# Chunk 0's phase A in two passes, and every second FFN weight cast on VectorE

## The reference

```python
# 1: mamba (inner width 2048)
xc, z = split(x @ W_in)                      # W_in 1024 x 4096
u  = silu(causal_conv4(xc))                  # per channel, 4 taps
dt_raw, B_raw = split(u @ W_x)               # 16 + 16 columns
dt = clip(softplus(dt_raw @ W_dt + b_dt), 1e-4, 1.0)
h_t = h_{t-1} * (1 - dt_t) + u_t * (B_raw @ W_Bp)_t
out = ((h + D_param * u) * silu(z)) @ W_out
# 2 and 4: ffn; the weights are int32 in -127..127, times 1/127, hidden width 3072
out = (silu(x @ wg.T) * (x @ wu.T)) @ wd.T
# 3: causal attention with K, V = split(x @ W.T), q = x, and its own residual
out = x + softmax(x @ K.T + mask) @ V
```

## Time and profile before

| | us |
|---|---|
| runs of the kernel | 3325.86, 3313.39; median 3319.63 |
| the profiled execution | 3315.65 |
| its span, first to last instruction, slowest core (core 1) | 3314.1 |
| spans of the 8 cores | 3288.6 to 3314.1 |
| busy: PE 1987.4, PE weight load 969.5, VectorE 954.4, ScalarE 776.3, GpSimd 323.3 | |

### The profile page before, as it was taken

One profiled execution on the slowest core, in us unless ns is written; L12 is line 12 of the kernel. 1 busy time (PEld: TensorE's weight loads), 2 busy tenths in 40 slices (PEclk: granted clock), 3 DMA queues, 4 the chain that ended last, 5 costly groups with the idle time before them and its releaser, 6 DMA issues.

```text
span 3314.1 us, 30059 instructions; the slowest of 8 cores (3288.6 to 3314.1 us)
## 1 busy us (share of the span) xinstructions
PE 1987.4 (60%) x9432; PEld 969.5 (29%) x9432; DVE 954.4 (29%) x1617; ACT 776.3 (23%) x1196; POOL 323.3 (10%) x404
## 2 busy tenths in 40 slices
PE   0355555555555531385776759514988486859587
PEld 0233333333333310131332324211434232324232
DVE  3244444444444440020211211053443121211121
ACT  0244545445454423300110101010011200101010
POOL 0222222122222210013000000000000000000000
PEclk9777666776767755697788989856999698989889
DMA  7200000000000018615112030344041512030303
GB/s 236 89 13 26 1 26 1 26 26 1 26 1 26 22 37 257 202 62 183 29 51 76 25 103 4 121 152 133 1 134 58 187 39 89 16 111 0 118 10 99
DMA packets 69851, 233.31 MB, mean 70 GB/s; under 512 B 8450, under 2 KB 8578, under 8 KB 67652
## 3 DMA queue, kind: packets, MB, share of 16 engines
q10 hardware_dynamic: 35712, 112.21, 10.2%
q1 hardware_dynamic: 27460, 91.92, 9.1%
q0 software_dynamic: 6528, 27.27, 2.0%
HBM read 170.55 MB, written 60.82 MB: 70 GB/s over the span
## 4 chain that ended last, share of the span: by engine, by line
PE 38%; DMA 22%; DVE 12%; ACT 9%; issue 8%; DVEq 4%; POOLq 3%; POOL 2%; ACTq 2%; SPq 0%
PE ps_s L974 15%; DMA arena<-wd_c 7%; PE ps_s L940 5%; DVEq L143 4%; DMA arena<-xs 4%; PE ps_s L1044 3%; PE ps L1044 3%; POOLq L143 2%; ACT L679 2%; POOL arena L560 2%; PE ps_s L1296 2%; DVE arena L516 2%; PE ps L759 2%; PE ps_s L1222 2%; DMA arena<-wu_t 2%
## 5 line engine op out<-in xcount | busy, mean ns | idle before, releaser
L974 PE MATMUL ps_s<-arena 128*128 128x512 bf16 x2304 | 511.7, 386 | 6.3 <-DVE arena L328 6.3
L584 PE MATMUL ps_s<-arena 128*128 128x256 bf16 x1024 | 214.1, 397 | 388.6 <-ACT arena L508 388.6
L318 PE MATMUL ps<-arena 128*128 128x128 bf16 x512 | 63.5, 307 | 488.7 <-DVE arena L307 488.7
L974 PEld LDWEIGHTS ps_s<-arena 128*128 128x128 bf16 x2304 | 228.1, 99 | 288.6 <-issue 25.8
L1044 PE MATMUL ps_s<-arena 128*128 128x512 bf16 x768 | 213.3, 401 | 135.9 <-DMA arena<-wd_c 89.4
L266 ACT ACTIVATE arena<-arena 128x1024 bf16<-128x1024 f32 x64 | 67.6, 1057 | 913.7 <-DMA arena<-xs 823.6
L584 PEld LDWEIGHTS ps_s<-arena 128*128 128x128 bf16 x1024 | 136.8, 138 | 458.0 <-issue 406.0
L940 PE MATMUL ps_s<-arena 128*128 128x512 bf16 x768 | 171.6, 387 | 122.2 <-ACT arena L950 63.5
L989 DVE TENSOR_TENSOR arena<-arena,ps_s 128x512 bf16<-128x512 f32 x144 | 99.0, 687 | 423.2 <-ACT arena L983 423.2
L1044 PE MATMUL ps<-arena 128*128 128x512 bf16 x768 | 212.5, 400 | 0.0
L499 PE MATMUL ps_s<-arena 128*128 128x256 bf16 x1024 | 163.2, 328 | 65.2 <-DVE arena L447 64.6
(11 more groups left out here) (93 smaller groups left out, 2347.7 us busy)
## 6 DMA issues: line engine op xcount, KB each, us to landing
xs<-arena ACTq DMA_DIRECT2D x48, 512.0 KB, 2.9
arena<-xs ACTq DMA_DIRECT2D x48, 512.0 KB, 4.3
arena<-wd_c SPq DMA_DIRECT2D x84, 256.0 KB, 2.6
arena<-wd_c ACTq DMA_DIRECT2D x84, 256.0 KB, 2.6
arena<-wg_t SPq DMA_DIRECT2D x16, 768.0 KB, 6.6
arena<-wu_t SPq DMA_DIRECT2D x16, 768.0 KB, 6.7
arena<-x ACTq DMA_DIRECT2D x16, 512.0 KB, 4.7
arena<-w_in ACTq DMA_DIRECT2D x8, 1024.0 KB, 10.6
```

What stands on the lines that cost most here:

```text
L318: lambda e, s=xn_bf_tile, dj=dj, pbf=pbf: e.transpose(pbf[:, dj * P:(dj + 1) * P], s[:, dj * P:(dj + 1) * P], g_ident),
L584: lambda e, dj=dj, ci=ci, bkx=bkx, half=half, par=par: e.matmul(psb[bkx][:, half * TCM:(half + 1) * TCM], win_bf[:, dj * 4096 + ci * P: dj ...
L974: lambda e, hi=hi, dj=dj, bk=bk, par=par, wsrc=wsrc: e.matmul(psb[bk], wsrc[:, dj * H + hi * P: dj * H + (hi + 1) * P], fxnt[par][:, dj * ...
```

## The change

Two edits. First, in chunk 0 all eight xc pairs of phase A are emitted, and then all eight z pairs. Second, while the gate and up weights are staged, the pieces of slot 1 are cast by VectorE (`tensor_copy`) and those of slot 0 by ScalarE as before. VectorE's cast waits for its load and for the ScalarE cast of slot 0 that goes with it, and SP's loads and GpSimd's stores then wait for VectorE's mark where they waited for ScalarE's.

```diff
         for p in range(8):
             phaseA_xc_pair(0, p)
-            phaseA_z_pair(0, p)
+        for zp in range(8):
+            phaseA_z_pair(0, zp)
         mk_xz_last = s_pe.mark()
         xp_sec(0)
         mamba_load_ln(1)
...
-                            em.op("scalar",
-                                  lambda e, dj=dj, hh=hh, dstw=dstw, slot=slot: e.copy(
-                                      dstw[:, dj * H + hh * 1536: dj * H + (hh + 1) * 1536],
-                                      stg[slot][:]),
-                                  wait=[mkd], inc=[(s_se, 1)], drain=False)
-                            prev2[slot] = mkk[dj] = s_se.mark()
+                            if slot == 0:
+                                em.op("scalar",
+                                      lambda e, dj=dj, hh=hh, dstw=dstw, slot=slot: e.copy(
+                                          dstw[:, dj * H + hh * 1536: dj * H + (hh + 1) * 1536],
+                                          stg[slot][:]),
+                                      wait=[mkd], inc=[(s_se, 1)], drain=False)
+                                prev2[slot] = s_se.mark()
+                            else:
+                                em.op("vector",
+                                      lambda e, dj=dj, hh=hh, dstw=dstw, slot=slot: e.tensor_copy(
+                                          dstw[:, dj * H + hh * 1536: dj * H + (hh + 1) * 1536],
+                                          stg[slot][:]),
+                                      wait=[mkd, prev2[0]], inc=[(s_ve, 1)],
+                                      drain=False)
+                                prev2[slot] = s_ve.mark()
+                            mkk[dj] = prev2[slot]
                             prev_cast[0] = mkk[dj]
```

## The result

| | before | changed |
|---|---|---|
| median of all runs | 3313.65 us (42 runs) | 3322.97 us (43 runs) |
| ratio | | 1.0027, 95% interval 1.0017 to 1.0038 |
| profiled execution, slowest core's span | 3314.1 us | 3315.3 us (core 4) |

The change makes the kernel slower by 0.27%, 8.9 us of 3313.65, with an interval from 5.6 to 12.6 us. The forecast was 6.1 us more, 0.18%. By the 2% bound it is no change.

A forecast was written before the change was run, and what follows sets the result against it. No single limit: a serial chain bounds phase A of chunk 0, transfers the weight stage. +9.6 us (first edit) and -3.5 (second) make +6.1, on the median of two runs, 3319.63, giving 3325.7 us; range 3311 to 3340.

The forecast's parts named there:

- The xc part: Phase A, chunk 0: an xc pair costs 5.95 us, 0.47 less than before; 3.7 us gained by the eighth SiLU.
- The z part without cover: Phase A, chunk 0: six z pairs left with nothing beside them; 11.4 us lost at full clock.
- clock term: Phase A, chunk 0: the z part begins at 1.2 GHz and loses 1.9 us, about half of such a stretch.
- No slack behind it: After phase A of chunk 0: chunk 1's loads, LayerNorm, transposes and first phase B matmul follow, so nothing absorbs the delay.
- (c): Rival: the first edit costs nothing, chunk 1's loads or the chunk behind having slack; -3.5 us in all; 5%.
- The cast on VectorE: Weight staging: a VectorE cast takes 0.96 us, 0.51 less than ScalarE's; 2 us counted of 7.7.
- 2 won and 2 lost: Weight staging: 2 us gained by the faster cast (0 to 7.7), 2 lost by slot 1's late first cast (0 to 4.7).
- The end of the stage: Weight staging: gate-phase SiLUs wait only for ScalarE's last cast, now slot 0's, so PE starts 3.45 us earlier.
- (a): Rival: weight staging is paced by latency, the shorter cast pays in full, -9.1 us there, +0.5 in all; 15%.
- (b): Rival: chunk 0's whole z part runs at 1.2 GHz, +17.7 us there, +14.2 in all; 12%.
- (d): Rival: both staging slots fall into step and the DMA engines idle during cast pairs; up to 55 us; 4%.
- (e): Rival: VectorE's casts wait and end no earlier than ScalarE's; +9.6 us stays, second edit near 0; 10%.

The follow-up runs named there:

- e2: The kernel before with only the second edit, slot 1's casts on VectorE, first run; ratio 0.9961 (0.9931 to 0.9990).
- e12: The kernel before with only the second edit, slot 1's casts on VectorE, run again; ratio 0.9986 (0.9966 to 1.0005).
- e5: The kernel before with all 16 casts of w_up on VectorE and all 16 of w_gate on ScalarE; ratio 0.9873 (0.9857 to 0.9888).
- e3: Second edit alone, but the first two casts both stay on ScalarE; edit against e2; ratio 0.9965 (0.9930 to 1.0001).
- e8_z_first_all: The kernel before with, in all 8 chunks, the z pair emitted ahead of its xc pair's last SiLU; ratio 0.9736 (0.9722 to 0.9749).

## Why the prediction was right

**The xc part: right.** 5.95 us a pair was predicted, 5.92 to 5.93 measured. The saving of one z SiLU per pair is real: the eighth L570 came 41.5 us after the first, 45.4 before, 3.9 us gained where 3.7 was forecast.

**The z part without cover: right, with luck in its clock term.** From the eighth L570 to the loads of x it takes 15.3 us on the core shown (162.98 to 178.32) where it took 1.2. As the mean of the cores it is 14.5 us, 13.3 more than before, and that is the 11.4 + 1.9 of the sum. The 1.9 was half of one row's low stretch. In the 32 blocks of the four kernels with edit 1 the low stretch lasts 2.9 to 6.1 us (matmuls start 0.21 us apart in it, 0.11 behind it) and costs 1.4 to 2.9 us. The reason that was given for it is off: the forecast took PE in the xc part for as thinly used as in the stretch from 1180, 1.91 of 5.95 us, but it worked 16.48 of 30 us with 0.65 granted (core 4, 128 to 158), and some blocks began at the full clock. The upper bound, all six pairs at 1.2 GHz, did not come. In the four kernels with edit 1 the interval to the first L659 has a mean of 69.7 us (69.4, 69.6, 69.9, 70.1), in before, e2, e12 and e5 60.1: 9.6 us, the number of the sum.

**No slack behind it: right.** Edit 1 alone gave 1.0035 in its second run, and the mean span of the cores grew by 8.5 and 10.1 us. Rival (c) is out.

**The cast on VectorE: right** in its duration (0.96 us), and by and large in what it pays. From the first cast to the end of the last nothing was gained or lost, 128.4 against 128.5 us, as 2 won and 2 lost had it; both 2s were choices inside a range. The two terms apart: the late first cast costs 2 to 3 us (e3 against e2 and e12). And with it gone, e3 shows the last cast ending 126.5 us after the first, 2.0 less than with all casts on ScalarE; 2 had been taken. The difference is from one execution and no larger than the scatter between executions. The reading that each ScalarE cast is at most a third of the time to the next is a little off: at the end of the earlier trace rows 1.47 us stand against 3.45. Nothing in the sum used it.

**The end of the stage: right in kind, a little smaller.** The SiLUs now wait for slot 0's cast. 3.45 us was called certain; the stages differ by 3.0, and by 5.1 in e3, where the late first cast is gone and 3.45 + 2 = 5.45 would be due. On the core shown slot 0's last cast begins 2.5 us before slot 1's, not 3.45: the distance between the slots is not fixed.

**The rivals.** (a), that a shorter cast pays in full, is out for the stage: 2.0 of 7.7 us came with the shorter cast and 7.1 of 16.7 were paid for the longer one. The stage of the changed kernel moved 292 and 303 GB/s in windows of 40 us at a DMA share of 0.88 and 0.91:

```profile
1264.00:1304.00 40.00, 0.00 (x0) 0.00 (x0) 4.80 (x5) 5.88 (x4) 3.15 (x6) 0.50 0.88 292
...
1340.00:1380.00 40.00, 0.00 (x0) 0.00 (x0) 4.80 (x5) 7.73 (x6) 2.66 (x5) 0.50 0.91 303
```

The Trainium skill, "DMA: Bandwidth & Descriptors", Specifications, gives about 358 GB/s as a core's share of HBM. These windows stay below it, and of the room that would be left a faster cast got only those 2.0 us. (b) and (d) did not come: the clock rose inside the z block, and the first loads, put out together (casts at 1262.21 and 1262.26), landed at different times, so that the slots were out of step again by the next casts (1268.12 on VectorE, ScalarE's next 3.4 us later). (e) is out by the VectorE casts' own rows.

**What is left over.** The two intervals of the changed kernel sum to 9.6 - 3.0 = 6.6 us; the ratio says 8.9 with an interval from 5.6 to 12.6. That is no contradiction. But edit 2 alone gained about 3 us more than its stage, which is not explained, and which would bring the sum of the parts down to 3 or 4 us; the changed kernel does not show it. So the terms of the two stages are shown, and the whole is known to a few us only. That the forecast time of 3325.7 lies 2.7 us from the measured median, 3322.97, is luck in part: the median of two runs on which it was built was 6.0 us above the median of 42, and the change on the medians was 3.2 us larger than forecast.

What the prediction did not see is not in its sum: it took both stages as they stood. It wrote that the SiLUs wait for ScalarE's queue only, and counted 3.45 us for it; the same sentence, followed one step further (keep all of w_up's casts out of that queue), was worth 42 us.

## What to carry to other kernels

Here the work that lay in the shadow of a serial chain through several engines cost only the instructions that it put into the chain's own queue; taken out of there it cost its full length, some of it at half the clock. So put it, and any table load that it brings, into the queue ahead of the instruction that waits, not behind it. When an engine's casts or copies stand in a queue, ask which consumer behind them does not need them: dividing the casts by consumer gave 42 us, dividing them evenly over two engines 3 in the stage.

## What the runs showed of the hardware

- ScalarE's table load takes 1.28 us each time, 57 times for the SiLU alone, and it can run in a wait: moved there it was free, 1.75 us less per pair together with the SiLU that moved (`e8_z_first_all`).
- After xc pairs in which PE worked 16.48 of 30 us with 0.65 of the clock granted (windows of the changed kernel, core 4, 128 to 158), a dense block began at 0.50 and stayed there for 5.3 us; at 1214.57 before, it had been 3.7 us. Over 32 such blocks, one per core and kernel, it was 2.9 to 6.1 us and cost 1.4 to 2.9 us. Some of the blocks began at 1.00 and fell to 0.50 within about 1 us, although they were dense.
- With a stage at a DMA share of 0.84 to 0.91, lengthening each cast by 1.04 us cost 43% of it, and the share fell to about 0.8. So here a share near 0.9 with two buffers in flight was a mixed limit.
